# Attention with a shared relative bias, then a gated channel mix, on one core: the softmax's division moved behind the mix

## The reference

```python
q, k, v = einsum('bsx,xMnd->Mbnsd', x, qkv)
a = einsum('bnsd,bntd->bnst', q, k) * 64 ** -0.5
bias = where(rel >= 0, cumsum(rpe_bias)[:, clip(rel, 0)], -30000.0)   # rel = query - key
a = softmax(a + bias, axis=-1)
mix = einsum('bnst,bntd->bnsd', a, v)
x = layernorm(x + einsum('bnsd,ndx->bsx', mix, out_w))
x_prev = x shifted by one token
xr, xk = mu_r * x + (1 - mu_r) * x_prev, mu_k * x + (1 - mu_k) * x_prev
x = layernorm(x + sigmoid(xr @ W_r) * (relu(xk @ W_k) ** 2 @ W_v))
```

## Time and profile before

| | |
|---|---|
| median of 3 runs | 1245.46 us (1243.8 to 1245.8) |
| the profiled execution | 1246.39 us |
| its span, first to last instruction | 1244.6 us |
| TensorE busy | 1118.1 us (90% of the span) |
| DVE busy | 843.3 us (68%) |
| ACT busy | 743.1 us (60%) |
| POOL busy | 886.9 us (71%) |
| the normalisations on POOL, 512 | 880.5 us, 1730 ns each |
| mean granted TensorE clock | 0.988 |
| DMA | 163.69 MB, mean 132 GB/s |

### The profile page before, as it was taken

The page is one execution under the profiler, slowest core; times in us unless marked ns, Lnnn a source line. Parts: engine busy times, 40 slices in busy tenths (PEclk is TensorE's granted clock), DMA queues, the critical chain, the costliest instruction groups (busy, mean ns, idle before and its releaser), DMA issues.

```text
span 1244.6 us, 21976 instructions
## 1 busy us (share of the span) xinstructions
PE 1118.1 (90%) x6909; PEld 781.9 (63%) x6909; DVE 843.3 (68%) x2505; ACT 743.1 (60%) x1857; POOL 886.9 (71%) x527
## 2 busy tenths in 40 slices
PE   5899999999999999999999999999999999999885
PEld 3666666666666666666666666666666666666664
DVE  2666666666676767777667777666777676777746
ACT  3666666666655656656665656665656566656623
POOL 1877777878876677876677876677876677776730
PEclk9899999999999999999999999999999999999997
DMA  8855445555655455655465654456654455654600
GB/s 199 208 122 124 115 117 122 130 132 134 157 138 115 116 141 127 160 137 129 116 141 132 159 127 118 117 140 153 159 123 115 123 134 142 155 122 110 213 18 20
DMA packets 101745, 163.69 MB, mean 132 GB/s; under 512 B 10592, under 2 KB 66288, under 8 KB 101632
## 3 DMA queue, kind: packets, MB, share of 16 engines
q1 hardware_dynamic: 99472, 161.37, 53.4%
q10 hardware_dynamic: 2160, 0.92, 0.3%
HBM read 41.63 MB, written 19.96 MB: 49 GB/s over the span
## 4 chain that ended last, share of the span: by engine, by line
PE 65%; DVE 17%; issue 8%; ACT 6%; POOL 2%; DMA 1%; DVEq 0%; SPq 0%; ACTq 0%
PE ps_o L946 21%; PE ps_t L930 15%; PE ps_rows L916 13%; PE ps_m L891 7%; DVE prob L615 4%; DVE pt L632 4%; PE ps_m L960 4%; PE ps_m L896 3%; ACT pt L474 2%; DVE mix_sb L638 2%; POOL prob L410 2%; ACT prob L463 1%; DVE k_lo L601 1%; DVE q_lo L601 1%; DVE shift L682 1%
## 5 line engine op out<-in xcount | busy, mean ns | idle before, releaser
L410 POOL TENSOR_SCALAR prob<-prob,inv 128x128 f32<-128x128 f32 (+7 forms) x512 | 880.5, 1730 | 308.2 <-DVE inv L622 306.2
L463 ACT ACTIVATE prob<-prob,low 128x128 f32<-128x128 f32 (+7 forms) x512 | 395.3, 773 | 119.1 <-DVE low L615 116.9
L615 DVE CUSTOM_DVE_ANT_0 prob<-ps_rows,table 128x128 f32<-128x128 f32 (+7 forms) x512 | 383.6, 749 | 72.7 <-PE ps_rows L916 66.2
L930 PE MATMUL ps_t<-ident,prob 128*128 128x128 f32 x2304 | 349.1, 278 | 87.2 <-ACT pt L474 50.1
L916 PE MATMUL ps_rows<-stacks 128*128 128x512 f32 (+3 forms) x1536 | 402.5, 372 | 4.6 <-DVE w_t L700 3.2
L930 PEld LDWEIGHTS ps_t<-ident,prob 128*128 128x128 f32 x2304 | 260.6, 141 | 198.3 <-issue 130.6
L632 DVE COPY pt<-ps_t 128x256 f32<-128x256 f32 (+2 forms) x320 | 179.1, 568 | 179.6 <-PE ps_t L930 178.8
L474 ACT ACTIVATE pt<-ps_t 128x128 f32<-128x128 f32 (+2 forms) x448 | 203.6, 477 | 110.8 <-PE ps_t L930 110.6
L946 PE MATMUL ps_o<-pt,v_pair 128*64 128x512 f32 (+3 forms) x1536 | 268.7, 492 | 0.0
L916 PEld LDWEIGHTS ps_rows<-stacks 128*128 128x128 f32 x1536 | 246.3, 191 | 22.7 <-DVE w_t L700 3.4
L946 PEld LDWEIGHTS ps_o<-pt,v_pair 128*64 128x64 f32 x1536 | 101.8, 136 | 181.8 <-issue 172.3
(11 more groups left out here) (108 smaller groups left out, 561.6 us busy)
## 6 DMA issues: line engine op xcount, KB each, us to landing
stacks<-k_hi SPq DMA_DIRECT2D x126, 256.0 KB, 4.7
stacks<-k_lo SPq DMA_DIRECT2D x126, 256.0 KB, 4.9
stacks<-q_hi SPq DMA_DIRECT2D x63, 256.0 KB, 3.7
stacks<-q_lo SPq DMA_DIRECT2D x63, 256.0 KB, 4.4
mix_transposed<-mix_sb SPq DMA_DIRECT2D x62, 256.0 KB, 2.0
table<-bias_by_distance SPq DMA_DIRECT2D x64, 192.0 KB, 3.7
mix_tile<-mix_transposed SPq DMA_DIRECT2D x24, 512.0 KB, 5.0
w_cur<-in_L_attn_qkv SPq DMA_DIRECT2D x31, 192.0 KB, 3.9
```

Of the source, the lines that this page charges most:

```text
L410: nc.gpsimd.tensor_scalar(row, row, inv[:, r:r + 1], None, ALU.mult).then_inc(s_norm, 1)
L463: nc.scalar.activation(row, row, ACT.Exp, bias=low[:, r:r + 1], scale=-1.0, accum_out=total[:, r:r + 1]).then_inc(s_exp, 1)
L615: nc.vector.tensor_tensor_reduce(prob[:, r % PSLOTS, 0:width], ps_rows[:, score_at(r):score_at(r) + width], table[n % 2][:, h, 0:width][:, ...
L930: ins = nc.tensor.transpose(ps_t[k % 2][:, P * b:P * b + P], prob[:, r % PSLOTS, at:at + P], ident[:, :])
```

## The change

**The division moves.** `normalise` is gone; the transposes wait for the exponential. The mix is made of rows that are not normalised, and `store_mix` multiplies it by `inv_all`, which holds the inverse sum of each query (along the free axis) for all 64 dimensions of a head (along the partitions). To get it there, DVE inverts the sums of 8 rows at a time (`invert(n, g)`, slots 5 and 12). TensorE transposes the eight columns into the unused end of bank 6 or 19 (`INV_BANK`); DVE (g = 0) or ACT (g = 1) copies the 8 x 128 to `inv_t`. SP writes it to DRAM (`store_inverse`) and reads it back as two broadcasts, each of four rows to 64 partitions (`spread_inverse`, 128 KB each).

**Tile steps on POOL.** The steps that touch SBUF alone (both layernorms' last operations, the token shift as six operations, the square) go from DVE to POOL; the second layernorm goes from slot 13 to 15. `CH` becomes 12, and `tile_store` waits for `s_out`.

**Copies.** From bank 15 on the copies alternate: banks 16, 18 and 22 go from ACT to DVE.

```diff
-EVACUATOR = "010110010100010111110111"
+EVACUATOR = "010110010100010101010101"
...
-V_PROJ, LN2_RSTD, LN2 = 12, 13, 13
+V_PROJ, LN2_RSTD, LN2 = 12, 15, 15
...
-CH = 13
+CH = 12
+INV_READY = (5, 12)
+INV_BANK = (6, 19)
...
+            def store_inverse(n, g):
+                sp.wait_ge(s_inv_t[g], n + 1)
+                sp.dma_start(inv_d[n % 2, g, :, :], inv_t[g][:, :]).then_inc(s_inv_d[g], 16)
+
+            def spread_inverse(n, g):
+                sp.wait_ge(s_inv_d[g], 16 * n + 16)
+                if n > 0:
+                    sp.wait_ge(s_o, 2 * n + g)
+                for h in range(2):
+                    sums = inv_d[n % 2, g, GROUP * h:GROUP * h + GROUP, :].rearrange("(a i) q -> a (i q)", a=1)
+                    sp.dma_start(inv_all[g][D * h:D * h + D, :], sums.broadcast_to([D, GROUP * P]))\
+                        .then_inc(s_inv_all[g], 16)
...
                 if n + 2 < PAIR_STEPS:
                     load_weights(n + 2)
+                if prev:
+                    spread_inverse(n - 1, 1)
...
                     store_mix(n - 1, 1)
+                store_inverse(n, 0)
                 if more:
                     sp.wait_ge(s_lo, 4 * n + 8)
                     for h in range(2):
                         stack_k(n + 1, h, s_stack[h])
+                spread_inverse(n, 0)
...
                 store_mix(n, 0) if more else None
+                store_inverse(n, 1)
...
-            for n in range(PAIR_STEPS):
-                for r in range(NROWS):
-                    normalise(n, r)
+            def tile_step(n, slot):
+                e = n - TILE_LAG
+                if slot == LN1:
+                    pool.wait_ge(s_chain, CH * (e + 1) + 3)
+                    pool.wait_ge(s_rstd, 2 * e + 1)
+                    nc.gpsimd.tensor_scalar(x1[:, :], y1[:, :], mv[:, 0, 0:1], rstd[:, 0:1],
+                                            ALU.subtract, ALU.mult).then_inc(s_chain, 1)
...
+            def invert(n, g):
+                rows = slice(2 * GROUP * g, 2 * GROUP * (g + 1))
+                dve.wait_ge(s_exp, NROWS * n + 2 * GROUP * (g + 1))
+                if n > 0:
+                    dve.wait_ge(s_tr, NBANKS * n + INV_BANK[g] + 1)
+                nc.vector.reciprocal(inv[:, rows], total[:, rows]).then_inc(s_inv, 1)
...
                 dve.wait_ge(s_mix_d[g], 16 * n + 16)
-                nc.vector.tensor_copy(mix_sb[g][:, :], ps_o[:, :]).then_inc(s_o, 1)
+                dve.wait_ge(s_inv_all[g], 32 * n + 32)
+                nc.vector.tensor_tensor(mix_sb[g][:, :], ps_o[:, :], inv_all[g][:, :], ALU.mult).then_inc(s_o, 1)
...
             def transpose(n, r):
-                pe.wait_ge(s_norm, NROWS * n + r + 1)
+                pe.wait_ge(s_exp, NROWS * n + r + 1)
...
+                    if k in INV_BANK:
+                        g = INV_BANK.index(k)
+                        pe.wait_ge(s_inv, 2 * n + g + 1)
+                        ins = nc.tensor.transpose(ps_t[k % 2][0:2 * GROUP, 3 * P:],
+                                                  inv[:, 2 * GROUP * g:2 * GROUP * (g + 1)], ident[:, :])
```

More of the change, by code:

```diff
@@ L130, in build @@
         inv = sb("inv", [P, NROWS])
+        inv_t = [sb(f"inv_t{g}", [2 * GROUP, P]) for g in range(2)]
+        inv_all = [sb(f"inv_all{g}", [P, GROUP * P]) for g in range(2)]
         pt = [[sb(f"pt{h}{g}", [P, GROUP * (g + 1), GROUP * P]) for g in range(2)] for h in range(2)]
@@ L203, in build @@
         s_inv = sem("inverted")
-        s_norm = sem("normalised")
+        s_inv_t = [sem(f"inverse_transposed{g}") for g in range(2)]
+        s_inv_d = [sem(f"inverse_in_dram{g}") for g in range(2)]
+        s_inv_all = [sem(f"inverse_broadcast{g}") for g in range(2)]
         s_tr = sem("transposed")
@@ L217, in build @@
         s_sig = sem("exp_gate")
+        s_out = sem("tile_finished")
+        s_gate1 = sem("gate_plus_one")
+        s_shift = sem("tokens_shifted")
         s_store = sem("stored")
@@ L404, in _ @@
             pool.memset(one[:, :], 1.0).then_inc(s_zero, 1)
-            def normalise(n, r):
-                width = P * (ROWS[r][1] + 1)
-                pool.wait_ge(s_inv, NROWS * n + r + 1)
-                row = prob[:, r % PSLOTS, 0:width]
-                nc.gpsimd.tensor_scalar(row, row, inv[:, r:r + 1], None, ALU.mult).then_inc(s_norm, 1)
-            for n in range(PAIR_STEPS):
-                for r in range(NROWS):
-                    normalise(n, r)
+            def tile_step(n, slot):
[5 more added lines that the diff above has]
+                                            ALU.subtract, ALU.mult).then_inc(s_chain, 1)
+                if slot == SHIFT:
+                    pool.wait_ge(s_x1t, e + 1)
+                    pool.wait_ge(s_mu, 1)
+                    at = e % TILES * P
+                    for a in range(2):
+                        nc.gpsimd.tensor_scalar(shift[:, a, :], x1_t[:, at:at + P], mu[:, 2 + a:3 + a], None,
+                                                ALU.mult).then_inc(s_shift, 1)
+                    for a, dst in enumerate((xr_t, xk_t)):
+                        nc.gpsimd.tensor_scalar(dst[:, :], x1_t[:, 1 + at:1 + at + P], mu[:, a:a + 1], None,
+                                                ALU.mult).then_inc(s_shift, 1)
+                    pool.wait_ge(s_shift, 4 * e + 4)
+                    for a, dst in enumerate((xr_t, xk_t)):
+                        nc.gpsimd.tensor_tensor(dst[:, :], dst[:, :], shift[:, a, :], ALU.add).then_inc(s_chain, 1)
+                if slot == RK_PROJ:
+                    pool.wait_ge(s_sig, e + 1)
+                    nc.gpsimd.tensor_tensor(k_act[:, :], k_act[:, :], k_act[:, :], ALU.mult).then_inc(s_chain, 1)
+                if slot == LN2:
+                    pool.wait_ge(s_rstd, 2 * e + 2)
+                    pool.wait_ge(s_store, 16 * e + 16)
+                    nc.gpsimd.tensor_scalar(o_tile[:, :], y3, mv[:, 1, 0:1], rstd[:, 1:2],
+                                            ALU.subtract, ALU.mult).then_inc(s_out, 1)
@@ L415, in _ @@
+            for n in range(TILE_LAG, PAIR_STEPS + 1):
+                for slot in range(NROWS):
+                    tile_step(n, slot)
             for w in range(TILES // WIDE):
@@ L461, in exps @@
                 act.wait_ge(s_biased, NROWS * n + r + 3)
+                if n > 0 and r % (2 * GROUP) == 0:
+                    act.wait_ge(s_inv, 2 * n - 1 + r // (2 * GROUP))
                 row = prob[:, r % PSLOTS, 0:width]
@@ L473, in evacuate @@
                 act.wait_ge(s_tr, NBANKS * (n + 1) + k + 1)
+                if k == INV_BANK[1]:
+                    if n > 0:
+                        act.wait_ge(s_inv_d[1], 16 * n)
+                    nc.scalar.activation(inv_t[1][:, :], ps_t[k % 2][0:2 * GROUP, 3 * P:], ACT.Copy).then_inc(s_inv_t[1], 1)
                 nc.scalar.activation(pt[h][g][:, b0:b0 + nb, P * (i % GROUP):P * (i % GROUP) + P],
@@ L707, in step @@
                         bias(*row)
-                    for row in rows_ahead(n, more, slot - 1):
-                        invert(*row)
+                    if slot in INV_READY:
+                        invert(n, INV_READY.index(slot))
                     if more and slot in PROJ_SLOTS[:4]:
@@ L799, in gated_sum @@
                 norm_stats(1, w, y3_l)
-            for slot in sorted({OUT_PROJ, LN1}):
-                tile_step(PAIR_STEPS, slot)
+            tile_step(PAIR_STEPS, OUT_PROJ)
             add_residual(0)
@@ L818, in _ @@
             gated_sum(0)
-            tile_step(PAIR_STEPS, LN2)
             log_gate(1)
```

39 lines of the change are left out of this document (10 added, 29 removed).

## The result

The changed kernel takes **1317.12 us** (median of 4 runs, 1316.03 to 1319.51) against 1244.83 for the kernel before on the same chip. The ratio is 1.0583, with a 95% interval of 1.0565 to 1.0602. The profiled execution took 1319.51 us, its span is 1317.8.

The account below looks back on a forecast made before the run. TensorE, busy 90% of the span, and its gaps were taken as the bound. Late broadcasts 56.1 and 17.1, transposes 4.5, tail -2 gave +75.7 on 1246.4, 1322.1; less 0.9 above the median, 1321 us, range 1254 to 1354.

Parts of the forecast that it names:

- Its first links: Slot 12: normalisations hidden; DVE held by row 15's reciprocal, then by the broadcast queued behind the k stacks, anew each step.
- The rival on the other side: Slots 13 to 15: ACT and DVE copy side by side, TensorE's end-of-step gaps close, 48.8 us; 1199 us, chance 0.09.
- The last link: Bank 18's copy behind DVE's wait makes TensorE's bank 20 2.55 us late in 22 steps with a tile: +56.1.
- the first rival: Broadcast lands by 632.35, DVE does not wait, bank 20 starts 0.2 us later in 31 steps: 1254 us, chance 0.08.
- POOL's row of 627.37 + 4.71: Rows 13 and 14 normalised by 632.08; removing normalisation alone would give row 13 at most 0.17 us, row 14 nothing.
- The landing: Near half's broadcasts, issued on SP behind the k stacks, land at 634.6, bounds 633.6 and 635.5.
- Without a tile: In 9 steps without a tile the broadcast lands at 266.5 and bank 22 is 1.9 us late: +17.1.
- The tail: After the steps, seven small operations leave DVE for POOL: -2 us, bounds -4 and 0.
- The residual sum: On DVE behind the product: 0.33 us off, from 0.609 us, with POOL's long operations gone.
- the transposes of the inverses: Two added to TensorE each step, 0.14 us each, one in a stretch that waits: +4.5 us.
- The gap before bank 10: TensorE's gap at 622.23, 0.77 us, was to stay, moving along with DVE's work.
- The wait before bank 20: TensorE's wait there was to grow from 0.7 to over 2 us and name DVE.

Follow-up runs that it names:

- Experiment 1: Changed kernel with the near half's two broadcasts issued between the k stacks of head 0 and head 1, not behind both: 1255.6 us.
- Experiment 5: Changed kernel with the near half's product at the end of slot 15 of DVE's queue instead of slot 12, broadcasts still behind all k stacks: 1256.8 us.
- experiment 4: Kernel before with the alternating copies alone: 1255.3 us.
- Experiment 3: Changed kernel with the copies as before, banks 16, 18 and 22 on ACT again: 1289.8 us.
- experiment 11: Kernel before, normalisation kept on POOL, with alternating copies, copies first in slots 12 to 15, near mix in slot 15, next input's load ahead of its store: 1224.5 us.
- Experiment 2: Changed kernel without the near half's two broadcasts and the wait on them, the product reading a constant: 1258.9 us.
- experiment 6: Changed kernel with broadcasts between the heads, near product in slot 15, and DVE's queue in slots 12 to 15 reordered with copies first: 1243.6 us.

## Why the prediction was right

**The mechanism.** Its first links held: the normalisations were hidden; DVE was held by row 15's reciprocal and then by the broadcast; the broadcast queued behind the k stacks; bank 18's copy stood behind that wait, and the delay came anew in each step. Experiment 1 moves the broadcasts ahead of half of the queue, and 62 of the 72 us are gone. Experiment 5 leaves them late and moves the product to slot 15, by when they have landed, and DVE no longer waits. The rival on the other side, the gaps close at 1199, is excluded by experiment 4: the alternation alone makes the kernel slower.

The last link was only half of it. The forecast led the delay to TensorE through bank 18's copy alone. The gate product stands behind the same wait, the value projection of slot 14 needs it, and by this way TensorE is already 1.92 us late ahead of bank 20. Experiment 3 takes bank 18's copy out of the chain, and 44.7 of the 72.3 us stay. The two ways run side by side, so leaving one out did not change the sum.

The price of the first rival, 1254, was met by luck: experiment 1 gives 1255.6, but as the sum of an alternation that costs 19 us, where about 6 had been reckoned (31 x 0.2), and of a rest that gains 9, where 2.5 had been added.

Two readings of the prediction are too tight, without an effect on the sum. POOL's row of 627.37 + 4.71 holds two normalisations; the first, of row 13, ends at 629.57, so that row has 2.7 us of slack and not 0.17. And POOL gets nine small operations a tile, not eight.

**The sum.** 1321 was forecast, 1317.1 measured. That it is so near is luck: errors of 18 and 15 us, and smaller ones, cancelled. From the trace, the span grew by 73.2 us: -1.5 before the first of these steps, +12.3 in 8 steps without a tile, +56.3 in the 22 steps with one, +6.1 from the last k stack to the end.

*The landing* was put too late. Forecast 634.6 in the frame of the step shown, measured 634.2 there and 633.8 in a step at full clock (product at 866.80, first k stack at 853.66, 13.14 us apart, as 633.84 is from 620.70). Both broadcasts together hold SP for 2.3 us, 1.16 each for 128 KB, but they land a little closer behind the stacks than the row of `x_res` said. Measured 1.67 us of wait each, forecast 2.3. So a step with a tile takes 39.33 us at full clock, 1.86 more than before, where 2.55 + 0.14 had been forecast: 0.8 us in 22 steps, 18 us too much. Without a tile it was 1.5 for 2.0.

*The clock* was not in the sum at all. Ten of the 22 steps with a tile take 40.9 us on average instead of 39.3, 15.5 us in all. Some 13 of these are the lower clock, the rest a later broadcast; that is told in the last section.

*The tail* was forecast 2 us shorter, since seven operations leave DVE. The stretch from the last k stack on is 6.1 us longer, and the cause lies in POOL's queue. First the changed kernel, then before:

```profile
1297.83 0.80 POOL L463 TENSOR_SCALAR o_tile<-shift,mv,rstd 128x128 f32<-128x128 f32 x1 [6.60 <-ACT rstd L548]
...
1299.68 2.08 PE L1099 MATMUL ps_rows<-w_t,prob 128*128 128x128 f32 x8 [7.18 <-POOL prob L473]
```

```profile
1226.53 2.07 PE L1051 MATMUL ps_rows<-w_t,prob 128*128 128x128 f32 x8 [2.33 <-POOL prob L418]
```

The last tile's second layernorm, moved to POOL, stands there ahead of the square of the last batch's first half and waits for `rstd`. TensorE stands 7.18 us for that square instead of 2.33: 4.85 us, in a term that had been forecast as a gain. The rest of the 6.1 was not followed.

**The smaller steps.** The residual sum went from 0.65 to 0.29 us, as taken. The Trainium skill (SBUF — State Buffer, "Who interferes with whom") says that a DVE instruction with two SBUF inputs contends with a GpSimd instruction that reads SBUF. The changed kernel fits that, since POOL is idle there, but experiment 4 does not:

```profile
635.43 5.34 POOL L410 TENSOR_SCALAR prob<-prob,inv 128x896 f32<-128x896 f32 x2
...
639.16 0.29 DVE L682 TENSOR_TENSOR shift<-y,x 128x128 f32<-128x128 f32 x1
```

There POOL reads SBUF all through the sum, and it takes 0.29 us, in 22 of 22 steps with a tile; experiment 11 has 0.27 beside POOL. So POOL at work is not enough to make it 0.65, and what is stays open. The square, with both inputs the same tile, takes 0.282 with POOL busy beside it. The product costs what the copy did (0.69). What the transposes of the inverses cost is not told apart: the step of experiment 1, 37.62 against 37.47, also holds the alternation's cost and the rest's gain. The gap before bank 10 stayed. The wait before bank 20 did not grow to over 2 us in one piece: 1.39 us of it lie ahead of the value projection and name `y`, 0.71 ahead of bank 20, where the row names ACT's exponential; bank 18's copy ended at 667.25, 0.15 before. The fit of the Trainium skill (DMA: Bandwidth & Descriptors, "Anatomy of one DMA — SWDGE (gpsimd) path") gives an estimate of 2.3 us for a broadcast. The page gives it for DMAs issued by GpSimd; these are issued by SP behind eight others, and 3.8 us were measured.

## What to carry to other kernels

A wait costs what stands behind it in the same in-order queue: the late broadcast cost 62 us with the product in slot 12, and with it in slot 15 DVE never waited for it. List every operation behind the wait that another engine needs, not only the first that comes to mind: here the way over the gate product was enough for the larger part of the loss. Before an engine's busy time is cut, look whether anything ever waits for it; here 880 us of POOL's work cost nothing, and experiment 11, which keeps them and changes DVE's order, the slot of the second layernorm, three copies and one issue on SP, is 21 us faster than the kernel before. Which of these does how much was not separated. Work moved to an idle engine stands in a queue there too: one operation of the tail cost 4.85 us on POOL. An issue moved on a DMA queue moves what is late behind it, so follow the next load each time (`x_cur`, then `mix_tile`).

## What the runs showed of the hardware

**TensorE's clock.** In the changed kernel the mean granted clock is 0.975 against 0.988. The windows of the step shown above:

```profile
653.00:663.00 10.00, 8.66 (x64) 6.55 (x63) 6.81 (x16) 5.46 (x13) 0.40 (x1) 1.00 0.95 211
...
663.00:667.30 4.30, 2.30 (x17) 1.79 (x16) 2.67 (x9) 1.14 (x5) 0.00 (x0) 1.00 0.73 217
...
667.30:671.30 4.00, 3.90 (x19) 3.59 (x20) 2.24 (x6) 1.94 (x6) 0.53 (x1) 0.57 0.01 2
...
671.30:682.00 10.70, 10.42 (x59) 6.04 (x57) 4.92 (x17) 5.29 (x16) 1.05 (x2) 1.00 0.32 87
```

From 667.3 to 671.3 the granted clock is 0.57: most of that stretch runs at the lower of its two levels, 1.2 GHz instead of 2.4. The transposes of banks 20 and 21 take 1.66 us for 7, those of 22 and 23 take 1.62 us for 8. Before it, TensorE had stood for 1.29, 1.39 and 0.71 us within 6 us. In a step that stayed at full speed it had stood for 1.29, 1.05 and 0.72, and the same transposes take 0.95 and 1.07 us:

```profile
865.47 0.85 PE L973 MATMUL ps_t<-ident,prob 128*128 128x128 f32 x6 [1.29 <-DVE pt L700]
...
867.83 1.13 PE L939 MATMUL ps_m<-w_cur,x_cur 128*128 128x128 f32 x8 [1.05 <-DVE y L734]
...
869.68 0.95 PE L973 MATMUL ps_t<-ident,prob 128*128 128x128 f32 x7 [0.72 <-ACT prob L520]
...
871.25 1.07 PE L973 MATMUL ps_t<-ident,prob 128*128 128x128 f32 x8
```

A step with such a stretch takes 1.55 us more (40.88 against 39.33). Of that the clock has about 1.29: of two steps in which TensorE stood 1.39 us for `y`, the one that begins at 570.67 reaches its output projection 19.07 us behind the first k stack, the one at 651.05 after 20.36. The rest, 0.26, is a later broadcast. Such stretches came in 10 of 22 steps with a tile in the changed kernel, in 10 of experiment 3, and in none of the kernel before or of experiment 1, where the gaps of a step's end add up to less (1.29 and 0.44). In the changed kernel the wait for `y` is 1.24 to 1.57 us in the ten and 0.98 to 1.39 in the others with a tile where it is named. Experiment 2 has one such step, after a gap of 1.64 us, and experiment 6 has them behind the wait of 3.15. So a stall can cost more than its length. That the stall brings the lower level is read from which steps have it; what decides between two nearly equal steps is left open.

**POOL's small operations.** With two scalars per partition, and two operations on each element, a 128 x 128 instruction takes longer than with one:

```profile
L463 POOL TENSOR_SCALAR o_tile<-shift,mv,rstd 128x128 f32<-128x128 f32 x24 | 19.1, 797 | 387.9 <-ACT rstd L548 387.9
...
L449 POOL TENSOR_SCALAR shift<-x_t,mu 128x128 f32<-128x128 f32 x48 | 28.4, 602 | 163.6 <-ACT x_t L553 163.6
```

0.80 us for the layernorm's (subtract, multiply) against 0.60 for a single multiply, where DVE took 0.34 for the first layernorm's. In the steps both were hidden; in the tail the layernorm's place in POOL's queue was not.
